# Layer 0 attention: the minimum with zero moves to ScalarE as a relu, and the softmax sums of a tile move behind the maxima of the next tile on VectorE

## The reference, cut to what matters

```
q = (query @ Wq + bq)   k = (key_value @ Wk + bk)   v = (key_value @ Wv + bv)     # 16 heads, D = 16
attn = einsum('bhqd,bhkd->bhqk', q, k) * scale
attn = clip(attn, -CLAMP, CLAMP)                 # CLAMP = 10000
attn = softmax(attn, axis=-1)                    # over 77 keys
x = einsum('bhqk,bhkd->bqhd', attn, v)
x = x + tanh(g_xattn[0]) * (x @ Wo + bo)
```

## Time and profile before

| | |
|---|---|
| median of 3 runs | 1357.1 us (1356.96 to 1358.56) |
| the profiled execution, its own time | 1351.81 us |
| its span | 1350.1 us |
| mean granted TensorE clock, share of 2.4 GHz | 0.949 |
| busy over the span: PE, DVE, ACT, POOL | 88%, 73%, 60%, 41% |
| layer 0 attention in the trace | from the start to about 324.5 us |

### The profile page before, as it was taken

One profiled execution on the slowest core, in us unless ns is written; L12 is line 12 of the kernel. 1 busy time (PEld: TensorE's weight loads), 2 busy tenths in 40 slices (PEclk: granted clock), 3 DMA queues, 4 the chain that ended last, 5 costly groups with the idle time before them and its releaser, 6 DMA issues. The chain is left out here.

```text
span 1350.1 us, 26442 instructions
## 1 busy us (share of the span) xinstructions
PE 1194.5 (88%) x8487; PEld 899.4 (67%) x8533; DVE 982.7 (73%) x2135; ACT 811.0 (60%) x2405; POOL 549.5 (41%) x594
## 2 busy tenths in 40 slices
PE   4989898996986499999999999957999999959898
PEld 3878797884543277777777777734777777735475
DVE  4998889793554166666666667736888888859898
ACT  2555545452654256665566665516777777829898
POOL 4666757573204222221111112116888888710000
PEclk9999999998887599999999999988999999979999
DMA  3223233223774325333333332236224242100033
GB/s 116 64 94 94 72 94 93 70 79 95 254 217 117 134 59 138 112 114 118 115 112 118 122 115 95 69 112 180 63 64 139 64 139 64 41 12 1 32 98 122
DMA packets 124158, 135.30 MB, mean 100 GB/s; under 512 B 13838, under 2 KB 108740, under 8 KB 123908
## 3 DMA queue, kind: packets, MB, share of 16 engines
q1 hardware_dynamic: 116577, 114.81, 27.6%
q0 software_dynamic: 6816, 18.62, 5.1%
q10 hardware_dynamic: 642, 0.33, 0.1%
HBM read 84.43 MB, written 49.29 MB: 99 GB/s over the span
## 5 line engine op out<-in xcount | busy, mean ns | idle before, releaser
L1403 ACT ACTIVATE exp_h<-exp_ps_h,exp_b_now 128x256 f32<-128x256 f32 x312 | 128.8, 463 | 159.4 <-PE exp_ps_h L1343 156.2
L1343 PE MATMUL exp_ps_h<-exp_xhi,exp_w_now 128*128 128x256 bf16 x1248 | 214.8, 276 | 4.4 <-DVE exp_xlo L1433 4.4
L1788 ACT ACTIVATE a_z<-a_ps_sc,a_nmx 128x77 f32<-128x77 f32 x512 | 159.2, 368 | 56.2 <-DVE a_nmx L1889 56.2
L1343 PE MATMUL exp_ps_h<-exp_xlo,exp_w_now 128*128 128x256 bf16 x624 | 172.1, 276 | 0.0
L1510 DVE TENSOR_TENSOR exp_hlo<-exp_h,exp_hhi 128x512 bf16<-128x512 f32 x156 | 106.7, 691 | 80.4 <-ACT exp_hhi L1407 77.1
L1355 PE MATMUL exp_ps_y<-moe_w2s,exp_hhi 128*128 x585 | 139.2, 379 | 2.0
L1343 PEld LDWEIGHTS exp_ps_h<-exp_xhi,exp_w_now 128*128 128x128 bf16 x1248 | 123.5, 99 | 20.6 <-issue 5.0
L1788 ACT ACTIVATION_READ_ACCUMULATOR a_z<-a_ps_sc,a_nmx 128x1 f32 x512 | 127.9, 250 | 0.0
L1311 POOL COPY exp_at_now<-all_token_of 128x2 int32<-128x2 int32 x39 | 8.4, 216 | 288.7 <-PE exp_ps_x L1330 273.2
L1755 PE MATMUL a_ps_o<-a_v_now,a_phi 128*128 128x256 bf16 (+1 forms) x640 | 106.5, 272 | 15.4 <-DVE a_plo L1878 15.4
L1407 ACT ACTIVATE exp_hhi<-exp_h 128x512 bf16<-128x512 f32 x156 | 98.3, 630 | 4.9
(11 more groups left out here) (245 smaller groups left out, 2959.7 us busy)
## 6 DMA issues: line engine op xcount, KB each, us to landing
a_stage<-in_L_ffn_W_dram SPq DMA_DIRECT2D x64, 256.0 KB
y_slots<-exp_y SPq DMA_DIRECT2D x78, 128.0 KB
fold_k<-route_kst SPq DMA_DIRECT2D x16, 308.0 KB, 4.3
fold_v<-route_vst SPq DMA_DIRECT2D x16, 308.0 KB
exp_job_in<-fold_k SPq DMA_DIRECT2D x14, 352.0 KB, 3.4
exp_job_in<-fold_v SPq DMA_DIRECT2D x14, 352.0 KB, 3.3
a_x<-in_x_dram SPq DMA_DIRECT2D x32, 128.0 KB, 2.4
x<-a_xo SPq DMA_DIRECT2D x32, 128.0 KB, 1.7
```

Of the source, the lines that this page charges most:

```text
L1343: mm = pe.matmul(ps_h[:, i, f % 2 * SLOT_T:(f % 2 + 1) * SLOT_T], w1_now[:, v, k, hl, f * P:(f + 1) * P], xx[:, k, :], start=(q == 0), sto ...
L1403: ins = act.activation(h[:, f, :], ps_h[:, i, f % 2 * SLOT_T:(f % 2 + 1) * SLOT_T], ACT.Gelu_apprx_tanh, bias=b1_now[:, v, f:f + 1])
L1788: ins = act.activation(z[:, u, h * KEYS:(h + 1) * KEYS], ps_sc[:, j, (h - SB[j][0]) * KEYS:(h - SB[j][0] + 1) * KEYS], ACT.Exp, bias=nmx[: ...
```

## The change

The DVE instruction min(z, 0) is removed. ScalarE now computes relu(-z), in place, and then exp(-scale * .), which is the same value: -relu(-z) = min(z, 0). The exp waits for the relu through the same semaphore `zc_done`, and the relu waits for `z_done`. On DVE, `sums(T - 1)` moves from before the residual of T-3 to between the three maxima of T and the clamp of those maxima.

```
@@ act, slot
                 if has(T - 1):
                     v = (t - 1) % 2
+                    act.wait_ge(s["z_done"], NSB * T)
+                    act.activation(z[:, v, :], z[:, v, :], ACT.Relu, scale=-1.0).then_inc(s["zc_done"], 1)
                     act.wait_ge(s["zc_done"], T)
-                    act.activation(z[:, v, :], z[:, v, :], ACT.Exp, scale=scale).then_inc(s["exp_done"], 1)
+                    act.activation(z[:, v, :], z[:, v, :], ACT.Exp, scale=-scale).then_inc(s["exp_done"], 1)
@@ dve, slot
                     block_values(T - 2, b)
-                if has(T - 1):
-                    sums(T - 1, (t - 1) % 2)
                 if has(T - SKEW):
...
                                           ALU.max).then_inc(s["max_done"], 1)
+                if has(T - 1):
+                    sums(T - 1, (t - 1) % 2)
+                if has(T):
                     dve.wait_ge(s["max_done"], NSB * (T + 1))
                     dve.tensor_scalar(mx[:, :], mx[:, :], -CLAMP / scale, CLAMP / scale, ALU.max,
                                       ALU.min).then_inc(s["mx_done"], 1)
...
-
-                    dve.wait_ge(s["z_done"], NSB * (T + 1))
-                    dve.tensor_scalar(z[:, u, :], z[:, u, :], 0.0, None, ALU.min).then_inc(s["zc_done"], 1)
```

## The result

The changed kernel takes 1386.9 us (median of 5, 1383.6 to 1387.7) against 1357.0 before (median of 5, 1354.8 to 1358.6): slower by 29.9 us, a ratio of 1.022, 95% interval 1.0204 to 1.0237. I had said 1387.9 in a range of 1378 to 1401, and slower with 95 in 100.

The account below looks back on a forecast made before the run. It took a closed loop through DVE as the bound, a second 0.23 us behind. Terms 28.7 + 1.0 + 1.0 + 1.2 - 1.1 = +30.8 on 1351.8 gave 1382.6, plus 5.3 to the median: 1387.9 us, range 1378 to 1401.

Parts of the forecast that it names:

- the first loop: Steady tile before: minimum, exp, sums, reciprocal, residual, maxima, clamp, z, closed through DVE; tile 8.24 us.
- The sums on the path, 1.55: Between maxima and clamp: the sums' and reciprocal's whole duration, less overlaps and a wake-up, enters the second loop, 1.55 us.
- the loop of 9.36: Changed steady tile: 3.18 from z to scores, 2.78 to maxima's end, 3.40 to z's end; 9.36 us for 8.24.
- The steady tiles, +28.7: The 23 steady tiles at 9.36 us each: 215.3 in place of 186.6, +28.7 us.
- Keys, +1.0: Three slots with keys: masking starts 1.15 sooner, 11.64 from z to z, +0.3 each, +1.0 us in all.
- Values, +1.0: Three slots with values: PE is the bound, 12.5 from z to z, +0.35 each, +1.0 us in all.
- Tiles 0 to 2, +1.2: First tiles: the same insertion of the sums twice, once hidden by the first values, +1.2 us.
- End, -1.1: Behind the last z: residual ahead of sums, values product starts earlier, last transposes at 315.6 not 316.62, -1.1 us.
- rival C: GpSimd's product beats the clamp, which then ends with it: +2.2 on 31 tiles, +69, 1457 us; 8 in 100.
- The product's chain: GpSimd's product, transposes, scores: scores could start at 6.2 to 6.6 against the loop's 6.58; 0 to 0.1 a tile at the high end.
- Rival A: DVE's load is the bound, so relieving it of 1.2 us makes tiles faster: 23 x -0.38 = -9, 1348 us; 3 in 100.
- Rival D: PE's new gaps bring the slow clock in each steady tile: +1.65 x 23 = +38, 1426 us; 4 in 100.

Follow-up runs that it names:

- experiment 8: The kernel before with the minimum left out and no relu, exp waiting for z_done, sums early: ratio 0.9888, -15.5 us.
- experiment 1: The changed kernel with the sums back in their old place, relu still on ScalarE: ratio 1.0054 to the kernel before, +7.4 us.
- 7: Sums in their old place, one whole-tile relu ahead of ScalarE's copy of the values product: ratio 1.0051 to the kernel before, +6.3 us.
- 6: Sums in their old place, relu in three pieces ahead of ScalarE's copy of the values product: ratio 0.9913 to the kernel before, -11.2 us.
- Experiment 5: The changed kernel with four spare reciprocals, so the clamp starts behind GpSimd's product: ratio 1.0846 to the kernel before, +116 us.
- experiments 3: The changed kernel with the relu left out, exp reading z directly, sums late: ratio 1.0146 to the kernel before, +19.6 us.
- 9: The changed kernel, sums late, with the relu in three early pieces ahead of ScalarE's copy: ratio 1.0108 to the kernel before.
- experiment 11: Relu on ScalarE, sums of the tile before moved behind z, last on VectorE: ratio 1.0701 to the kernel before, +96 us.

## Why the prediction was right, point by point

- **Which loop binds.** Said: not DVE's load, but the chain z, relu, exp, q, scores, maxima, sums, clamp, z. Shown: the relu alone gained nothing, the sums alone brought the steady tile to 9.3 to 9.4, and each link stands in the timeline above: 3.18 from z to the scores as said, 2.88 from the scores' start (232.57) to the maxima's end where I had 2.78, and 3.26 from there to the end of z where I had 3.40, 9.32 in all.
- **What bounded the kernel before: one link misread.** I ran the first loop through the residual, the maxima and the clamp on DVE, and read beside it that the clamp waits for GpSimd's product. It is that wait which closes the loop. In rows 3, 4 and 7, z ends at 208.26, the product starts at 212.62 and ends at 214.87, the clamp ends at 214.90 and z at 216.50. The loop is minimum, exp, sums, reciprocal, product, end of the clamp, z. Residual and maxima have room in it: the clamp takes 0.17 to 0.19 where nothing holds it, and 0.43 here, so about 0.25. The same sum gives the tile of each kernel with its sums ahead of the residual, except that of experiment 8, whatever DVE's load:

| | z's end to product's start | product's start to next z's end | tile |
|---|---|---|---|
| before | 4.36 | 3.88 | 8.24 |
| relu alone (experiment 1) | 4.50 to 4.57 | 3.89 | 8.39 to 8.46 |
| one relu, ahead of the copy (7) | 4.49 | 3.89 | 8.38 |
| relu in three pieces (6) | 3.81 | 3.89 | 7.70 |

```profile
206.69 1.57 DVE L597 SCALAR_TENSOR_TENSOR a_z<-a_ps_sc,a_mx 128x462 f32<-128x462 f32 x3
```

This is why DVE's freed 1.2 us was worth nothing. The loop is read from the rows of these four kernels; no run moved the clamp ahead of the product with the sums left early, which would test it directly. It did the forecast no harm: the changed kernel has the clamp ahead of the product, and its loop is the other one, as said.
- **The relu, 1.23.** It took 1.23, with 0.04 ahead and 0.03 behind.
- **The sums on the path, 1.55, and the loop of 9.36.** Measured 9.24 to 9.32. The sum of the sums' terms is 1.56 and not 1.55, which changes nothing. The clamp took 0.11 and not 0.19, and the part from the maxima to z came out 0.14 shorter; the maxima, 0.10 later, took most of that back in the tiles of 9.32.
- **The steady tiles, +28.7.** 290.0 in all, less keys and values (below), leaves 213.7 for 23, against 186.6 to 186.8: +27.
- **Keys, +1.0.** The three slots took 38.8 against 38.9 by the rows of the kernel before (my sum had 39.0): -0.1. The masking starts sooner as said, and the slot without a slow clock took 11.40 where I had 11.64. The slow clock fell on other slots: it was the second and third before; now it is the first and third, where it adds 4.6 and not 5.1. This is the window in the first one, with its clock:

```profile
96.00:100.00 4.00, 2.91 (x14) 2.94 (x15) 1.94 (x8) 1.82 (x3) 2.83 (x4) 0.54 0.00 0
```

- **Values, +1.0.** 12.5 from z to z said, 12.51 to 12.52 measured, 1.0 more than before in the three.
- **Tiles 0 to 2, +1.2.** Measured +2.6 (z of tile 2 at 46.87 against 44.27). This term was mis-sized. 0.8 of it was there before any of the change acts (z of tile 0 at 25.86 against 25.06, behind a later load of x); the rest is 1.8.
- **End, -1.1.** The last output projection's residual ends at 353.49 against 324.49, +29.0; z of tile 31 starts 30.4 later, so the end gained 1.4. The values product that waited 3.08 for the residual now waits 0.58 for a copy, and the last transposes wait for the product:

```profile
341.94 2.72 PE L422 MATMUL a_ps_vo<-a_pT,a_vblk 128*128 128x128 f32 x22 [0.58 <-ACT a_pT L480]
...
345.90 1.31 PE L391 MATMUL a_ps_p<-all_ident,a_z 128*128 128x128 f32 x10 [1.23 <-POOL a_z L317]
```

- **The sum.** 2.6 + 27.8 (29 intervals) - 1.4 = 29.0 in the stage. The spans differ by 31.7; the other 2.7 lie in later stages that the change doesn't touch, and the medians differ by 29.9. That these agree to 1 us with +30.8 is in part luck, from errors of both signs: the steady tiles were 2 us less, the keys slots 1 us less, the first tiles 1.4 us more, the later stages 2.7 us more. The 5.3 us from the profiled time to the median, which I carried along, measured 3.3. The low end of the range took a relu of 1.05 as halfway to 0.80; halfway is 1.02, which would put it at 1377.
- **The clamp first, rival C.** Right, and by 0.16 (237.00 against 237.16). Experiment 5 shows that behind the product it would have cost 1.9 a tile. The Trainium skill (SBUF — State Buffer, "Who interferes with whom") has the rule that the first to issue keeps the other out for its whole length; for the product ahead of the clamp the traces agree (clamp 1.99, ending with the product, where it takes 0.11 when it comes first). That a clamp ahead keeps the product out no run shows: in the run with one spare reciprocal the product starts 0.05 behind the clamp and takes 2.25 as everywhere.
- **The product's chain.** I had it up to 0.4 behind, or level. It is about 0.45 behind: the tile without a relu is 8.81, 0.43 to 0.51 under the changed kernel's. It cost nothing here, but it caps every cure that leaves the sums late (experiments 3 and 9).
- **Rival A.** The Trainium skill (Perfetto Trace Analysis, "Optimizing Scalar/DVE Operations") says that offloading from a saturated VectorE to ScalarE may help. Here it helped only once the moved work ran under the work that feeds it: +7.4 us in one piece, -11.2 us in three.
- **Rival D.** PE's gaps of 0.99 and 0.25 left the clock at 1.00 in all steady tiles looked at (windows 46 to 96 and 104 to 260). In experiment 11, with waits of 2.80 to 2.90 in each tile, it was 0.86 in one tile (169.64 to 181.95) and 1.00 in the next two (181.95 to 203.19).

What stays open: why tiles in the middle of the stage take 9.32 and at its start and end 9.24 (the 0.08 lies between the end of q and the start of the scores, which begin 3.18 after z in place of 3.10), and which gaps of nearly 3 us are followed by a slow clock and which are not.

## What to carry to other kernels

Before moving work off a busy engine, write out the closed loops of one steady tile and look at which of them the moved piece stands in: an engine busy for 7.8 of 8.2 us was relieved of 1.2 us and nothing was gained, while reordering 1.7 us of its work cost 1.1 us a tile. A step on the loop pays when it runs in pieces under its producer, as the relu in three pieces did, and it pays only down to the next bound, here the loop through GpSimd's product at 7.70 us, with TensorE at 7.60 just under it. Close the loops through waits that no semaphore orders as well: two rows that end together on two engines, tile after tile, are a sign of a link. And an engine that the profile shows busy without a gap need not be the bound; leaving the work out tells. When a result also feeds a slower side chain (here sums to GpSimd's product to transposes), placing it late makes that chain the next bound.

## What the runs showed of the hardware

- A 16-column VectorE tensor_scalar on SBUF took 0.11 us when it started 0.05 to 0.16 us ahead of a GpSimd tensor_tensor of 2.25 us, and 1.99 us, ending with it, when it started 0.28 us behind it. The GpSimd instruction took 2.25 us each time.
- Four reciprocals of 128x16 in a row took 0.53 us together though one takes 0.25: these short VectorE instructions, with no wait between them, overlapped by more than half here.
- A relu on ScalarE took as long as an exp of the same size, 1.23 us for 128x1232, and three pieces took 1.48 us together.
- TensorE showed busy for 30.79 of 30.79 us in tiles of 7.70 us and for 22.80 of 22.80 us with the same matmuls in tiles of 7.60 us. The difference shows only in the length of the scores, 2.34 us against 2.24 us.
